# Who makes the inflow of state 6: TensorE, or GpSimd and VectorE by tile

## What is computed

```
def step(h, inp):
    u_t, d_t, b_t, c_t = inp
    dA  = exp(d_t[..., None] * A)                    # decay
    dBu = (d_t * u_t)[..., None] * b_t[:, None, :]   # inflow
    h   = dA * h + dBu
    y   = einsum('bdn,bn->bd', h, c_t)
```

## Time and profile before

| | |
|---|---|
| median of three runs | 5066.4 us |
| profiled execution | 5063.64 us, span 5061.9 us |
| scan part of the span | 204.7 to 4264.3 us, 2048 scans |
| PE (TensorE matmul) busy | 4436.9 us, 88% |
| DVE (VectorE) busy | 3837.9 us, 76% |
| POOL (GpSimd) busy | 3594.8 us, 71% |
| ACT (ScalarE) busy | 3408.0 us, 67% |

### The profile page before, as it was taken

The page is one execution under the profiler, slowest core; times in us unless marked ns, Lnnn a source line. Parts: engine busy times, 40 slices in busy tenths (PEclk is TensorE's granted clock), DMA queues, the critical chain, the costliest instruction groups (busy, mean ns, idle before and its releaser), DMA issues. The chain is left out here.

```text
span 5061.9 us, 73875 instructions
## 1 busy us (share of the span) xinstructions
PE 4436.9 (88%) x25304; PEld 3269.4 (65%) x25304; DVE 3837.9 (76%) x4157; ACT 3408.0 (67%) x5699; POOL 3594.8 (71%) x3035
## 2 busy tenths in 40 slices
PE   1689989898989898999999999998999998898998
PEld 0366666666666666666666666666666675686786
DVE  4488888989898989898989898989898996212212
ACT  1477777777777777776767676767677774663653
POOL 1378787878787878786878787878787896432422
PEclk9799999999999999999999999999999999999999
DMA  5202020202020202020202020202020110313313
GB/s 217 76 1 85 9 85 9 85 9 85 9 82 12 81 13 80 13 81 13 81 13 81 13 80 14 80 14 73 21 64 30 54 36 13 125 59 110 106 51 116
DMA packets 276891, 288.26 MB, mean 57 GB/s; under 512 B 87376, under 2 KB 166864, under 8 KB 274992
## 3 DMA queue, kind: packets, MB, share of 16 engines
q1 hardware_dynamic: 268080, 266.91, 16.7%
q10 hardware_dynamic: 8448, 16.78, 0.9%
HBM read 246.38 MB, written 37.26 MB: 56 GB/s over the span
## 5 line engine op out<-in xcount | busy, mean ns | idle before, releaser
L743 POOL TENSOR_TENSOR hs<-hs,c_rows 128x512 f32<-128x512 f32 x2048 | 2397.3, 1185 | 698.7 <-DVE hs L690 680.0
L690 DVE TENSOR_TENSOR_SCAN hs<-da,carry,bank 128x512 f32<-128x512 f32 x1152 | 1465.0, 1272 | 325.3 <-issue 137.0
L779 PE MATMUL bank<-b_diag,du_t 128*128 128x128 f32 x9216 | 1267.9, 281 | 360.1 <-DVE hs L690 339.0
L779 PEld LDWEIGHTS bank<-b_diag,du_t 128*128 128x128 f32 x9216 | 1147.2, 195 | 483.2 <-DVE hs L690 343.8
L879 PEld LDWEIGHTS bank<-identity,hs 128*128 128x128 f32 x8192 | 994.4, 142 | 610.1 <-issue 542.1
L479 ACT ACTIVATE da<-delta,neg_a 128x512 f32<-128x512 f32 x1152 | 826.7, 719 | 664.2 <-DVE hs L690 662.7
L879 PE MATMUL bank<-identity,hs 128*128 128x128 f32 x8192 | 1170.3, 274 | 4.2 <-POOL hs L743 2.4
L690 DVE TENSOR_TENSOR_SCAN hs<-bank,carry,hs 128x512 f32<-128x512 f32 x896 | 1111.1, 1262 | 1.2 <-POOL hs L737 0.5
L479 ACT ACTIVATE bank<-delta,neg_a 128x512 f32<-128x512 f32 x896 | 610.7, 686 | 149.8 <-DVE xs L647 93.0
L1049 POOL TENSOR_TENSOR xg_low<-xg,xg_high 128x512 fp32r<-128x512 f32 x192 | 248.6, 1295 | 476.5 <-ACT xg_high L1073 469.0
L810 PE MATMUL bank<-xn,w_in 128*128 128x512 f32 x1024 | 518.7, 603 | 23.4 <-DVE xs L632 12.3
(11 more groups left out here) (160 smaller groups left out, 5965.9 us busy)
## 6 DMA issues: line engine op xcount, KB each, us to landing
c_rows<-b_and_c_rows SPq DMA_DIRECT2D x256, 256.0 KB, 7.4
xl<-x SPq DMA_DIRECT2D x48, 1024.0 KB, 5.6
b_diag<-b_diagonals SPq DMA_DIRECT2D x144, 256.0 KB, 7.5
b_rows<-b_and_c_rows SPq DMA_DIRECT2D x112, 256.0 KB, 7.0
c_rows<-in_x SPq DMA_DIRECT2D x8, 2048.0 KB, 8.1
xn<-in_x ACTq DMA_DIRECT2D x16, 1024.0 KB, 9.6
xres<-in_x SPq DMA_DIRECT2D x64, 256.0 KB, 3.6
x<-xres SPq DMA_DIRECT2D x64, 256.0 KB, 2.0
```

What stands on the lines that cost most here:

```text
L690: dve.tensor_tensor_scan(state(n), decay, inflow, carry[:, STATE * j + n:STATE * j + n + 1], ALU.mult, ALU.add).then_inc(h_ready, 1)
L743: pool.tensor_tensor(weighted(n), state(n), c_rows[:, n, :], ALU.mult).then_inc(hc_ready, 1)
L779: mm = pe.matmul(x_ps[ring_bank(nn)][:, q * P:(q + 1) * P], du_t[:, jn % 2, q * P:(q + 1) * P], b_diag[:, w, q, :], start=True, stop=True)
```

## The change

State 6 leaves BY_TENSOR. In tiles 0 to 5 GpSimd makes its inflow, at slot 4, behind its product of state 3 and ahead of that of state 4. In tiles 6 and 7 VectorE makes it, at slot 5, ahead of the scan of state 5. Its B row is loaded as a row and not as a diagonal, so there are eight DMAs onto the diagonals in place of nine, and its decay goes to a PSUM bank in place of `da`. The waits count inflows by a function of the tile now.

```diff
--- before.py
+++ after.py
@@ -24,11 +24,26 @@
 H_RING, X_RING, CARRIES = 8, 3, 4
 BLOCKS = T // P
 
-BY_VECTOR = (2, 5, 8, 11, 14, 15)
-BY_TENSOR = (0, 1, 4, 6, 7, 9, 10, 12, 13)
-BY_POOL = (3,)
-ROWS = BY_VECTOR + BY_POOL
-N_V, N_T, N_P = len(BY_VECTOR), len(BY_TENSOR), len(BY_POOL)
+BY_TENSOR = (0, 1, 4, 7, 9, 10, 12, 13)
+ROWS = (2, 3, 5, 6, 8, 11, 14, 15)
+N_T = len(BY_TENSOR)
+POOL_TILES = 6
+
+
+def by_pool(j):
+
+    return (3, 6) if j % JT < POOL_TILES else (3,)
+
+
+def by_vector(j):
+    return tuple(n for n in ROWS if n not in by_pool(j))
+
+
+def inflows(states, tile, n=-1):
+
+    per_chunk = sum(len(states(j)) for j in range(JT))
+    before = sum(len(states(j)) for j in range(tile % JT))
+    return per_chunk * (tile // JT) + before + sum(1 for s in states(tile) if s <= n)
 
 
 
@@ -432,10 +447,11 @@
 
                             if n in ROWS:
                                 v = ROWS.index(n)
-                                if n in BY_VECTOR:
-                                    wait(sp, dbu_ready, N_V * (JT * (c + 1) - 1) + v + 1)
+                                last = JT * (c + 1) - 1
+                                if n in by_vector(JT - 1):
+                                    wait(sp, dbu_ready, inflows(by_vector, last, n) if c >= 0 else 0)
                                 else:
-                                    wait(sp, pool_dbu, N_P * (JT * (c + 1) - 1) + BY_POOL.index(n) + 1)
+                                    wait(sp, pool_dbu, inflows(by_pool, last, n) if c >= 0 else 0)
                                 sp.dma_start(b_rows[:, v, :],
                                              bc_d[n:n + 1, :].partition_broadcast(P)).then_inc(b_loaded[v], 16)
                             if n in BY_TENSOR:
@@ -578,7 +594,7 @@
                                     act.activation(du_t[:, jn % 2, :], x_ps[DU_BANK][:, :], ACT.Copy).then_inc(du_t_ready, 1)
                                 if n == DU_COPY:
                                     act.wait_ge(du_ready, nt + 1)
-                                    wait(act, dbu_ready, N_V * nt)
+                                    wait(act, dbu_ready, inflows(by_vector, nt))
                                     act.activation(du_ps[:, :], du[:, :], ACT.Copy).then_inc(du_copied, 1)
                             if n == Y_COPY and ((scan and j > 0) or (project and j == 0)):
                                 act.wait_ge(n_summed, STATE * tile)
@@ -663,10 +679,10 @@
                             def carries_done(back):
                                 return STEPS // CARRIES * c + (slot + back) // CARRIES + 1
 
-                            if scan and n + 1 in BY_VECTOR:
+                            if scan and n + 1 in by_vector(j):
                                 nn = n + 1
-                                v = BY_VECTOR.index(nn)
-                                if v == 0:
+                                v = ROWS.index(nn)
+                                if nn == by_vector(j)[0]:
                                     dve.wait_ge(du_copied, tile + 1)
                                 if j == 0:
                                     dve.wait_ge(b_loaded[v], 16 * (c + 1))
@@ -676,11 +692,11 @@
                                                   ALU.mult).then_inc(dbu_ready, 1)
                             if scan:
                                 dve.wait_ge(da_ready, step + 1)
-                                if n in BY_VECTOR:
-                                    dve.wait_ge(dbu_ready, N_V * tile + BY_VECTOR.index(n) + 1)
+                                if n in by_vector(j):
+                                    dve.wait_ge(dbu_ready, inflows(by_vector, tile, n))
                                     decay, inflow = x_ps[ring_bank(n)][:, :], state(n)
-                                elif n in BY_POOL:
-                                    dve.wait_ge(pool_dbu, N_P * tile + BY_POOL.index(n) + 1)
+                                elif n in by_pool(j):
+                                    dve.wait_ge(pool_dbu, inflows(by_pool, tile, n))
                                     decay, inflow = x_ps[ring_bank(n)][:, :], state(n)
                                 else:
                                     dve.wait_ge(dbu_mm, N_T * tile + BY_TENSOR.index(n) + 1)
@@ -717,7 +733,7 @@
                                 wait(pool, xs_ready, JT * cn + jn + 1)
                                 wait(pool, du_turned, nt)
                                 wait(pool, du_copied, nt)
-                                wait(pool, pool_dbu, N_P * nt)
+                                wait(pool, pool_dbu, inflows(by_pool, nt))
                                 settle(pool, pool_fence)
                                 pool.tensor_tensor(du[:, :], delta[:, jn % 2, :], xs[:, cn % 2, jn, :],
                                                    ALU.mult).then_inc(du_ready, 1)
@@ -728,7 +744,7 @@
                                 settle(pool, pool_fence)
                                 pool.tensor_tensor(xs[:, o % 2, jp, :], xs[:, o % 2, jp, :], zs[:, :],
                                                    ALU.mult).then_inc(gated, 1)
-                            if scan and n + 2 in BY_POOL:
+                            if scan and n + 2 in by_pool(j):
                                 nn = n + 2
                                 if j == 0:
                                     pool.wait_ge(b_loaded[ROWS.index(nn)], 16 * (c + 1))
```

## The result

The changed kernel takes 5110.1 us (median of 4 runs, 5107.9 to 5110.7), the kernel before 5066.0 beside it: ratio 1.0088, interval 1.0070 to 1.0105. It is 0.9% slower. The forecast was 5067, range 5048 to 5092. Its sum held in almost every tile, as will be seen, and its end was wrong, because it took TensorE's granted clock as given.

What follows compares the result with a forecast made beforehand. VectorE's scans were taken as the path, broken by waits for GpSimd, TensorE or ScalarE. Terms of +0.03 per chunk (14 times, +0.4), +3.6, -2.3 and -1.5 summed to +0.2 us: 5067 us, range 5048 to 5092.

Steps and rivals of the forecast that it cites:

- tile 0: In each middle chunk, GpSimd's added inflow makes du later and the whole delay counts: +1.23 us.
- tile 2: TensorE, without a pause there, brings the scan of state 7 and the skip earlier by its dropped group: -0.89 us.
- tile 3: The scan of state 6 no longer waits for TensorE's group, but the convolution's first tap limits the gain: -0.39 us.
- tile 6: VectorE's added multiplication delays the scan of state 5, then ScalarE's logarithm, du and state 12: +0.55 us.
- tile 7: TensorE comes earlier, but du limits the gain at state 12: -0.47 us.
- tiles 1, 4 and 5: GpSimd's addition fits into its free time and the waits for ScalarE or VectorE stay: 0 us.
- The first scan: Ahead of chunk 0, one fewer DMA onto the diagonals lets the first inflow start earlier: -2.3 us.
- chunk 0: In its tile 0 TensorE, at the lower clock, no longer waits for state 6's diagonal: -1.5 us, between 0 and 3.
- a second stretch of 0.50 in each chunk: Sign of being wrong: granted TensorE clock at 0.50 (1.2 GHz) a second time in each chunk.
- The rival of the lull ahead of du: Tile 0's TensorE lull grows from 0.83 to 2.95 us, clock falls, up to 1.7 us per chunk: 5091 us; chance 0.18.
- The damped chunk: Tile 1's fixed low-clock stretch absorbs half of a delay, chunk stays at 256.0 us; shares 0.50 with no change.
- The last chunk: Tiles 0, 4 and 5 +1.23 each, 3 +0.9, 2 +0.7, 1 -0.9, 7 -0.8, 6 at 0: sum +3.6 us.

Runs made afterwards that it cites:

- before_delay: Kernel before with 10 matmuls by zeros (1.08 us) added in tile 0 at slot 11 of chunks 0 to 14: 5108.4 us, ratio 1.0085.
- before_fill: Kernel before with 12, 24 and 16 matmuls by zeros in TensorE's three pauses (two in tile 1, one in tile 3): 5057.9 us, ratio 0.9975.
- before_once: Kernel before with 10 matmuls by zeros (1.08 us) in tile 0 of chunk 4 alone: 5066.1 us, ratio 0.9999.
- pool_1to5_fill: Changed kernel with VectorE making state 6 in tile 0 too, and five TensorE pauses in tiles 1, 3 and 5 filled: 5060.6 us, ratio 0.9980.
- pool_1to5: Changed kernel with VectorE making state 6 in tile 0 as well, GpSimd in tiles 1 to 5: 5103.0 us, ratio 1.0076.
- before_minus: Kernel before with three of the four matmuls of state 6's inflow left out, result not valid: 5081.5 us, ratio 1.0036.
- after_fill: Changed kernel with 12, 24 and 16 matmuls by zeros in TensorE's three pauses in tiles 1 and 3: 5063.2 us, ratio 0.9997.
- after_fill_t3: Changed kernel with 16 matmuls by zeros in TensorE's pause of tile 3 alone: 5091.7 us, ratio 1.0038.

## Why the prediction was wrong

**The engines' terms held.** In chunks without a fall each is there: tile 0 +1.09 (forecast 1.23), tile 2 -0.89 (-0.89), tile 3 -0.39 (-0.39), tile 6 +0.55 (0.55), tile 7 -0.40 (-0.47), tiles 1, 4 and 5 nothing. Such a chunk changes by -0.04. The first scan came 0.9 earlier in place of 2.3, chunk 0 was 2.6 shorter in place of 1.5: together 3.5 against 3.8. That these two agree is partly luck. The eight DMAs took 18.29 us against 20.33 for nine, but they began 1.67 later, and the sum has no term for that. And the first scan lies anywhere from 197.7 to 208.1 us in these 14 traces (204.7 and 206.8 in two that have the same code up to there but for three matmuls), so one trace can't tell 0.9 from 2.3.

**The step that failed** is tile 1 at 0 and tile 3 at -0.39, and in the last chunk tiles 0, 1 and 4: all took it that TensorE's other work runs at the clock it had before. The prediction wrote that pauses of about 2 us in tiles 3 and 5 "were passed at full clock", and took this for a property of the pauses. before_delay shows that it was not: the same pause of 1.87 us in tile 1 and of 1.96 in tile 3 brings the clock down, in half of the chunks, when it comes a microsecond later. The trace of the kernel before had it already. Its chunk 7, which the prediction read, passes both pauses; chunk 1 doesn't pass the first, and chunk 8 not the second:

```profile
492.93 1.68 PE L779 MATMUL bank<-b_diag,du_t 128*128 128x128 f32 x8 [1.87 <-DVE hs L690]
...
493.40:496.80 3.40, 3.40 (x10) 2.02 (x9) 2.41 (x3) 0.29 (x1) 3.01 (x3) 0.50 0.27 77
...
2373.89 1.88 PE L779 MATMUL bank<-b_diag,du_t 128*128 128x128 f32 x8 [1.96 <-DVE hs L690]
...
2374.10:2377.50 3.40, 3.40 (x12) 2.26 (x12) 3.18 (x4) 2.18 (x5) 3.40 (x3) 0.51 0.01 2
```

What the prediction named as a sign of being wrong, a second stretch of 0.50 in each chunk, is what came. Chunks 1 to 14 are 42.5 us longer without the filling and 3.0 with it, so at least 39.5 of the 42.5 are falls; of the 3.0 some 2.5 are the two falls in tile 6. What a fall costs, by the tiles of chunks with and without it: late in tile 1, 3.4 us long, 0.2 (before against before_fill); the same, 6.8 long, 0.3 to 0.9 in tile 1 and 0.9 in tile 2; at the start of tile 1 0.8 to 1.8; in tile 3 1.7 (34.7 to 36.4, 35.1 to 36.8); in tile 5 at slot 8 1.7, at slot 2 nothing; in tile 6 1.3. So the number of low stretches doesn't tell the price. Where the timelines were read, in tiles 1 and 3, it is what VectorE waits longer for.

**The rival of the lull ahead of du** had the mechanism and the sign, and a chance of 0.18, but in chunks 1 to 14 the wrong place. The pause there grew to 1.55 and not to 2.95, and tile 0 kept its clock in all 14. The sum of 0.83, 0.89 and 1.23 took it that TensorE would be through 0.89 earlier with its work ahead of du. It was 0.3 later (17.66 us behind the chunk's start, against 17.35), since it now stood 1.14 for a scan on the way. The price of 1.7 per chunk is what one fall in tile 3 cost; the falls were several, and 3.0 came. In the last chunk the rival had the place too, as follows.

**The damped chunk** is refuted as it was put. The chunk didn't stay at 256.0. There is something in it: chunks of several versions settle at repeated lengths, 256.0 and 259.4 above all, before_once returns to 256.0, and a second microsecond cost next to nothing. But the next length up is 3.4 us away, and a delay of 1.1 was enough to go there.

The Trainium skill (TensorE: Matmul & The Clock Gate, What's actually happening) says that the watch on TensorE's activity runs freely and doesn't start with the kernel; by it the same pause can be passed or not, as it falls. The runs agree: the pause of 1.87 us was passed at 1.00 in the kernel before and followed by 0.51 in the one after, in chunk 7 of both, and in the kernel before alone it was both, in chunks 7 and 1. The prediction used the rule that busy share counts, and left this one out.

**The last chunk** cost 7.2 in place of 3.6, and this too comes with falls of the clock. Tile by tile it changed by +2.39, +0.65, +0.65, +0.77, +2.35, +1.16, -0.02 and -0.77; the forecast was +1.23, -0.9, +0.7, +0.9, +1.23, +1.23, 0 and -0.8. What was missed is tiles 0, 1 and 4. Tile 4 of the kernel before, then tiles 4 and 5 of the kernel after with the stretches around tile 4's du, and TensorE there:

```profile
4159.40:4185.60 26.20, 21.03 (x156) 17.53 (x155) 23.82 (x25) 19.76 (x33) 25.76 (x23) 1.00 0.00 2
...
4203.00:4231.50 28.50, 22.00 (x147) 18.13 (x146) 23.96 (x25) 19.68 (x33) 26.90 (x24) 0.94 0.00 1
4231.50:4258.90 27.40, 20.46 (x148) 16.58 (x147) 23.97 (x26) 19.78 (x33) 26.94 (x24) 1.00 0.00 1
...
4219.00:4222.40 3.40, 0.95 (x7) 0.60 (x6) 1.92 (x2) 0.72 (x1) 3.40 (x4) 1.00 0.01 2
4222.40:4225.80 3.40, 3.40 (x18) 3.40 (x17) 0.94 (x1) 1.97 (x4) 3.40 (x4) 0.50 0.00 0
...
4222.16 0.90 PE L780 MATMUL bank<-identity,du 128*128 128x128 f32 x4 [2.45 <-POOL du L738]
4222.86 1.91 PE L795 MATMUL bank<-b_diag,du_t 128*128 128x128 f32 x8
```

GpSimd's additional inflow makes tile 5 1.16 longer, as forecast (1.23). Tile 4 has the same addition and the same pause ahead of du, 2.45 us (before 1.64; tile 5 2.46), but there the clock falls behind it, and that is the other 1.2: in pool_1to5_fill, where it doesn't fall in tile 4, the tile takes 27.4 with the same pause. Tile 0 is like tile 4. Tile 1 has a fall at its start; in pool_1to5, where it has none, it is 0.9 shorter than before, as forecast. The last chunk of before_minus takes 216.1 as the kernel before does, but that hides both sides: a fall at the start of tile 1 costs 1.0, and tiles 2 and 7 are 0.9 shorter. after_fill, in which the last chunk is not filled, has the same three falls and 223.4.

**What stays open.** What sets a chunk on one of its lengths was seen twice (0.3 us more in a tile), and what these 0.3 us are is not known. No run filled the pauses ahead of du in the last chunk, so its share of the clock is read from tiles with and without a fall, and not produced. Why tile 0 gives back only half with VectorE on state 6 was not followed up.

## What to carry to other kernels

Where TensorE is near the path and has pauses of about 2 us, read the granted clock of each tile, in several chunks and not in one, for a shift of 1 us elsewhere can cost three. A chunk of another length in the trace of the kernel before, here chunk 8, is a warning. Before judging a small change there, fill the pauses in both versions with matmuls that change nothing, and compare those: here that brought back each term of a middle chunk to within 0.25 us, and to within 0.15 in chunks without a fall, and was faster by itself. Fill pauses only; the same matmuls in TensorE's busy stretches cost 70 us.

## What the runs showed of the hardware

The same code in one execution took 256.0 and 259.5 us per chunk, and the tiles that differ are those with falls of the clock (after_fill_t3). A pause of 1.87 us was passed at the granted clock of 1.00 in one chunk and followed by 0.50 in another of the same execution (before, chunks 7 and 1). Taking away 0.67 us of TensorE's work per tile made the kernel before 18 us slower (before_minus), and adding 52 useless matmuls per chunk made the changed kernel 47 us faster (after_fill). Transposing matmuls by zeros are enough to keep the clock up: with 12, 24 and 16 of them in the three pauses, tiles 1 and 3 had no fall in any of 14 chunks. In a row a transposing 128x128 matmul takes 0.109 us at full clock.
